# Second gather of a graph layer: one of 32 row blocks is fetched by SyncE, row by row, instead of by a GpSimd gather

## The chip, the cores and the metric

The kernel runs on one core of a Trainium2 chip. The metric is the device time of one execution in microseconds (us); lower is better. The core has five engines with a queue each: TensorE (PE, with its weight loads as PEld), VectorE (DVE), ScalarE (ACT), GpSimd (POOL) and SyncE (SP). SP computes nothing: it issues transfers and waits on semaphores. Its sequencer's work, like that of the other engines, is marked with a q (SPq).

## The reference, cut to what matters

The reference normalises 12,500 node rows of 256 floats, adds two branches to them, and then a layer of experts:

```python
def _gcn_layer(x, W, b, edge_weight, edge_src, edge_dst):
    support = x @ W
    msgs = support[edge_src] * edge_weight[:, None]
    agg = jax.ops.segment_sum(msgs, edge_dst, num_segments=N_NODES)
    return agg + b
...
h = jax.nn.elu(_gcn_layer(x, W1, b1, edge_weight, edge_src, edge_dst))
h = jax.nn.elu(_gcn_layer(h, W2, b2, edge_weight, edge_src, edge_dst))
...
xn = _layernorm(x, axis=-1)
x = x + _L0_gnn_ref(xn, ...) + _L0_mix_ref(xn[None], ...)[0]
x = x + _L0_ffn_ref(_layernorm(x, axis=-1)[None], ...)[0]
```

There are 212,500 edges, sorted by their destination. A graph layer fetches a source row of 1 KB for every edge, weighs it and adds it to its destination's row. The mix branch (`_L0_mix_ref`) is a linear attention with a two-layer network over all nodes.

## The kernel before, in words

The program is a chain of stages: `prepare` (layer norm and tables), `gather` for the first graph layer, `gather` for the second, `route`, `scatter` and `experts`. The change touches the second `gather`.

A gather stage goes through the edges in 104 turns of 2048 edges. A turn has 16 slots, each a block of 128 rows, one per partition. Turns alternate between two buffers, `u` = 0 (even turns) and `u` = 1 (odd turns); all loops run over pairs of turns, 52 in all. In a turn:

- POOL waits until the turn's indices are there (`idx_loaded`) and until its row buffer is free (`rows_used`), then issues one indirect transfer for each slot (line 451). `rows_used` of a buffer is raised by PE's first product of the next turn, so POOL can fill a buffer only while PE works on the other.
- DVE builds selection matrices `sel` (line 403) from the edges' destinations and weights.
- PE multiplies rows by selections (line 395) for four windows of four slots each, into `sums`. Ahead of the first and third windows it waits for that half of the turn's rows. Between the windows it does pieces of the mix branch and of the dense part of a finished node tile; after the fourth it does the hidden layer of the mix (line 983).
- DVE adds the four windows into `agg` (line 409), then raises `turn_added` (line 508), on which PE waits before the next turn's first window.
- SP, in its own turn, waits until all rows of the buffer's last turn have landed (line 421), loads the next indices (line 422), loads the next tile of the mix, stores the mix's result (lines 915 to 918: wait for the result, store, wait for the store, release the result buffer), and then stores and loads for the dense part (lines 1268 to 1276). It issues eight transfers in a turn.

No scheduler is at work: each engine's order is the order in which its block is written.

Of the kernel before, what the change touches and what calls it, by code (L numbers as in the profile page):

```python
# [6 lines left out]
I32 = mybir.dt.int32  # L7
# [5 lines left out]
P = 128  # L13
# [40 lines left out]
AGG = SPARE + WIN  # L54
TABLES = "natural_log_exp_and_others"
LOG_WIN = 6
LOG_TB = 8
# [32 lines left out]
def load_values(nc, engine, of, most):  # L90

    return nc.values_load_multi_w_load_instructions(of, engines=(engine,), min_val=0, max_val=most)[1]


# [15 lines left out]
def prepare(nc, m):  # L110

    with ExitStack() as ctx:
# [68 lines left out]
        with nc.Block("prepare") as block:  # L181
# [41 lines left out]
            @block.gpsimd  # L223
            def _(pool):
                nc.gpsimd.memset(m.zeros[:, :], 0.0).then_inc(zero_set, 1)
                nc.gpsimd.memset(m.ones[:, :], 1.0).then_inc(zero_set, 1)
                nc.gpsimd.iota(iota_i[:, :], [[1, WIN]], base=0, channel_multiplier=0).then_inc(iotas_done, 1)
                nc.gpsimd.iota(node_i[:, :], [[P, NT]], base=0, channel_multiplier=1).then_inc(iotas_done, 1)
                nc.gpsimd.iota(taken[:, :], [[0, 1]], base=(1 - LAG) * P, channel_multiplier=P).then_inc(taken_ready, 1)
                pool.wait_ge(zero_set, 2)  # L230

                nc.gpsimd.affine_select(out=m.ident[:, :], in_=m.zeros[:, 0:P], compare_op=ALU.not_equal, fill=1.0,
                                        base=0, pattern=[[-1, P]], channel_multiplier=1).then_inc(iotas_done, 1)
                nc.gpsimd.affine_select(out=m.upto[:, :], in_=m.ones[:, :], compare_op=ALU.is_ge, fill=0.0,
                                        base=0, pattern=[[1, P]], channel_multiplier=-1).then_inc(iotas_done, 1)
# [12 lines left out]

            @block.vector
            def _(dve):  # L250
# [54 lines left out]
                normalise(loops - 1, PSLOTS - 1, False)  # L305
                dve.wait_ge(iotas_done, 4)
                nc.vector.tensor_copy(m.cols[:, :], iota_i[:, :]).then_inc(tables_done, 1)
# [33 lines left out]

def gather(nc, m, layer, source, mixer, denser):

# [3 lines left out]
    with ExitStack() as ctx:  # L347
# [22 lines left out]
        sums = ps("sums", TURN * KD, WIN).rearrange("p (g k) w -> p g k w", g=TURN)  # L370

        idx_loaded = [sem(f"idx_loaded{u}_") for u in range(2)]
        rows_loaded = [[sem(f"rows_loaded{u}{b}_") for b in range(BANKS)] for u in range(2)]
        rows_used = [sem(f"rows_used{u}_") for u in range(2)]
# [36 lines left out]
        with nc.Block(f"gather{layer}") as block:  # L411
            @block.sync
            def _(sp):
                for u in range(2):
                    sp.dma_start(idx[:, u, :], m.in_src[u]).then_inc(idx_loaded[u], 16)
                    mix.load(sp, u, u)
                mix.load_weights(sp)
                dense.load_weights(sp)

                def turn(i, u):  # L420
                    sp.wait_ge(rows_loaded[u][BANKS - 1], 16 * GROUP * SUB * i)
                    sp.dma_start(idx[:, u, :], m.in_src[bass.ds(2 * i + u, 1)].rearrange("o p c -> (o p) c")
                                 ).then_inc(idx_loaded[u], 16)
                    mix.free(sp, i - 1, u)
                    mix.load(sp, 2 * i + u, u)
                    mix.store(sp, i - 1, u)
                    dense.sp(sp, i - 1, u)

                for i in range(1, dense.peeled):
                    for u in range(2):  # L430
                        turn(i, u)
                with sp.Fori(dense.peeled, loops) as i:
                    for u in range(2):
                        turn(i, u)
                mix.load_past(sp)
                for u in range(2):
                    dense.sp(sp, loops - 1, u)
                mix.stored(sp)
# [93 lines left out]
            def _(pe):  # L532
# [5 lines left out]
                def turn(i, u):  # L538
# [6 lines left out]
                    for g in range(TURN):  # L545
                        if g % SUB == 0:
                            pe.wait_ge(rows_loaded[u][g // SUB], 16 * GROUP * SUB * (i + 1))
# [175 lines left out]
def keys_values(nc, m, sb, sem, ps, shared):  # L723
# [110 lines left out]
    mix.dve, mix.act, mix.after = dve, act, after  # L834
    mix.store = lambda sp, i, u: None
    mix.load_weights = load_weights
# [4 lines left out]
def attend(nc, m, sb, sem, ps, shared):  # L841
# [70 lines left out]

    def store(sp, i, u):
        t = 2 * i + u
        sp.wait_ge(mixed, t + 1)
        sp.dma_start(m.mix[bass.ds(t * P, P), :], result[:, u, :]).then_inc(stored[u], 16)
        sp.wait_ge(stored[u], 16 * i + 16)
        sp.sem_inc(result_free[u], 1)

    def load_past(sp):  # L920
# [4 lines left out]
    def all_stored(sp):  # L925
        for u in range(2):
            store(sp, TURNS // 2 - 1, u)

# [183 lines left out]

    mix.load, mix.free, mix.store, mix.stored = load, free, store, all_stored
    mix.pe_begin, mix.pe, mix.pe_end = pe_begin, pe, pe_end
# [314 lines left out]
def route(nc, m):  # L1429


    with ExitStack() as ctx:
# [27 lines left out]
        spare_i = sb("spare_i", [P, NT], I32)  # L1460
        spare_f = sb("spare_f", [P, NT])
        blocks_i = sb("blocks_i", [1, NE], I32)
        blocks_f = sb("blocks_f", [1, NE])
# [17 lines left out]
        with nc.Block("route") as block:  # L1481
            @block.gpsimd
            def _(pool):
                nc.gpsimd.iota(left_i[:, :], [[-1, NE]], base=NE, channel_multiplier=0).then_inc(iotas, 1)
                nc.gpsimd.iota(spare_i[:, :], [[P, NT]], base=TRASH, channel_multiplier=1).then_inc(iotas, 1)
# [7 lines left out]
            def _(pe):  # L1493
                pe.wait_ge(chosen_ready, 1)
                for k in range(2):
                    half = chosen[:, k * HALF:(k + 1) * HALF, :]

                    nc.tensor.matmul(nth_ps[k], m.upto[:, :], half, start=True, stop=True)
                    nc.tensor.matmul(count_ps[k], m.ones[:, :], half, start=True, stop=True).then_inc(counted, 1)

            @block.vector
            def _(dve):
                count = [0]

                def link(instruction):
# [7 lines left out]
                                        ALU.subtract).then_inc(shifted, 1)  # L1513
                dve.wait_ge(iotas, 2)
                nc.vector.tensor_copy(left_f[:, :], left_i[:, :])
# [379 lines left out]
def program(nc, ins, out, scratch):  # L1895
    m = Memory()
    (m.x, m.in_src, m.in_dst, m.in_dst_rows, m.in_wgt, m.in_w_g1, m.in_b_g1, m.in_w_g2, m.in_b_g2,
     m.in_w_q, m.in_w_k, m.in_w_v, m.in_w_m, m.in_w_1, m.in_w_2, m.in_ln1_g, m.in_ln1_b, m.in_ln2_g, m.in_ln2_b,
# [12 lines left out]
    with ExitStack() as ctx:  # L1911
# [15 lines left out]
        m.ident = sb("ident", [P, P])  # L1927
        m.upto = sb("upto", [P, P])
        m.ones = sb("ones", [P, P])
# [16 lines left out]
        with ExitStack() as agg_ctx:  # L1946
            m.agg = agg_ctx.enter_context(nc.sbuf_tensor("agg", [P, KD, AGG], F32))
            gather(nc, m, 1, m.xn, keys_values, dense_first)
            gather(nc, m, 2, m.h1, attend, dense_second)
        m.row = sb("row_of", [P, NT], I32)  # L1950
# [51 lines left out]
```

## Time and profile before

| what | us |
|---|---|
| median of 3 runs (5253.92 to 5268.12) | 5263.27 |
| the profiled execution, its own time | 5257.51 |
| span of its trace, first to last instruction | 5255.6 |

The span is what the trace shows, and the 1.9 us beside it lie outside of the trace. The second gather's products run from about 2300 to 4425 us of the span. The stretch from 2500 to 4200 us is taken below as its steady part.

### The profile page before, as it was taken

How to read it: one execution, taken by the hardware profiler on the slowest of the kernel's cores; microseconds unless marked ns; L12 is line 12 of the kernel's file. 1: busy time of each engine (PE TensorE's matmuls, PEld its weight loads, DVE VectorE, ACT ScalarE, POOL GpSimd, SP SyncE). 2: the span in 40 equal slices, each digit the busy share in tenths (PEclk: the TensorE clock that was granted, in tenths of full speed). 3: DMA queues.
4: the chain of work that ended last, by engine and by line, in shares of the span. 5: the costliest groups of instructions: out<-in, count | busy, mean ns of one | idle time of the engine just before them, and what ended most of it. 6: DMA issues, size and time to landing. Idle time of an engine off the chain costs nothing. (4 is left out here: it accounts for less than half of the span.)

```text
span 5255.6 us, 89454 instructions
## 1 busy us (share of the span) xinstructions
PE 4074.3 (78%) x25266; PEld 3747.3 (71%) x25267; DVE 2650.4 (50%) x9578; ACT 814.5 (15%) x2507; POOL 3445.0 (66%) x3639
## 2 busy tenths in 40 slices
PE   0577777777777777769988999898989987069998
PEld 0467666666667776758888888888888886058886
DVE  7433333333333333355676666767666666234444
ACT  2001111111111111111222222222222222011111
POOL 0577777777777777757777777777777774632222
PEclk9867777777777777778999999999999998589999
DMA  7444444444444444434555454555545553632221
GB/s 212 142 128 132 130 132 132 130 132 130 132 131 133 132 130 132 129 89 125 147 147 152 143 151 145 147 149 146 151 144 148 147 146 109 188 112 70 67 70 65
DMA packets 409075, 693.81 MB, mean 132 GB/s; under 512 B 108237, under 2 KB 275661, under 8 KB 408893
## 3 DMA queue, kind: packets, MB, share of 16 engines
q0 software_dynamic: 177312, 488.43, 32.8%
q1 hardware_dynamic: 195765, 163.17, 10.6%
q10 hardware_dynamic: 35920, 41.25, 2.2%
q8 instruction: 40, 0.66, 0.0%
q14 instruction: 38, 0.31, 0.0%
HBM read 562.84 MB, written 129.68 MB: 132 GB/s over the span
## 5 line engine op out<-in xcount | busy, mean ns | idle before, releaser
L395 PEld LDWEIGHTS sums<-sel,rows 128*128 128x128 f32 x13312 | 1888.7, 222 | 768.0 <-DMA rows<-xn,idx 440.8
L395 PE MATMUL sums<-sel,rows 128*128 128x64 f32 x13312 | 1894.5, 305 | 672.9 <-DMA rows<-xn,idx 354.6
L451 POOL DMA_INDIRECT rows<-xn,idx x1664 | 1577.8, 948 | 642.4 <-issue 630.8
L451 POOL DMA_INDIRECT rows<-h,idx x1664 | 1585.3, 953 | 578.5 <-issue 528.9
L403 DVE TENSOR_SCALAR sel<-cols,rel_now,wgt_now 128x64 f32<-128x64 f32 x3360 | 780.4, 336 | 7.8
L409 DVE TENSOR_TENSOR agg<-agg,sums 128x128 f32 x832 | 240.3, 289 | 783.9 <-issue 604.7
L603 DVE TENSOR_TENSOR pre<-z,b_g 128x256 f32<-128x256 f32 x98 | 41.6, 424 | 526.8 <-PE z L598 526.8
L1807 PE MATMUL y_ps<-w,e_hidden 128*128 128x256 f32 x1248 | 286.1, 389 | 0.0
L1795 PE MATMUL e_hidden_ps<-tokens_t,w 128*128 128x256 f32 x1248 | 279.2, 381 | 4.4 <-DVE e_hidden L1864 3.6
L983 PE MATMUL hidden_ps<-xt,w 128*128 128x128 f32 x1664 | 265.2, 282 | 17.2 <-ACT msg_t L1104 17.0
L1735 POOL DMA_INDIRECT out<-y_result,target_i x80 | 79.5, 994 | 291.3 <-DVE y_result L1849 271.3
L1795 PEld LDWEIGHTS e_hidden_ps<-tokens_t,w 128*128 128x128 f32 x1248 | 237.5, 191 | 40.0 <-DVE e_hidden L1864 6.6
L1807 PEld LDWEIGHTS y_ps<-w,e_hidden 128*128 128x128 f32 x1248 | 241.8, 196 | 33.3
L983 PE MATMUL hidden_ps<-msg_t,w 128*128 128x128 f32 x1664 | 254.2, 275 | 0.0
L983 PEld LDWEIGHTS hidden_ps<-xt,w 128*128 128x128 f32 x1664 | 221.3, 193 | 35.3 <-ACT msg_t L1104 35.3
L946 PE MATMUL row_ps<-w,hidden 128*128 128x256 f32 x832 | 223.6, 418 | 2.7 <-ACT hidden L1108 2.7
L983 PEld LDWEIGHTS hidden_ps<-msg_t,w 128*128 128x128 f32 x1664 | 219.7, 192 | 0.0
L779 PE MATMUL kv_proj<-w_k,kv_xt 128*128 128x256 f32 x416 | 210.0, 660 | 0.0
L795 DVE TENSOR_SCALAR k_min<-kv_proj 128x256 f32<-128x256 f32 x104 | 44.1, 424 | 302.3 <-PE kv_proj L779 302.3
L946 PEld LDWEIGHTS row_ps<-w,hidden 128*128 128x128 f32 x832 | 170.1, 215 | 26.1 <-ACT hidden L1108 2.9
L971 PE MATMUL row_ps<-w_m,msg_t 128*128 128x256 f32 x416 | 125.4, 426 | 71.2 <-ACT msg_t L1096 71.2
L779 PE MATMUL kv_proj<-w_v,kv_xt 128*128 128x256 f32 x416 | 174.8, 567 | 0.0
(211 smaller groups left out, 4547.4 us busy)
## 6 DMA issues: line engine op xcount, KB each, us to landing
xe<-zeros ACTq DMA_DIRECT2D x104, 258.0 KB, 4.1
rows<-xn,idx POOLq DMA_INDIRECT x1664
rows<-h,idx POOLq DMA_INDIRECT x1664
w<-in_ffn_w POOLq DMA_DIRECT2D x16, 1024.0 KB
tile<-xn SPq DMA_DIRECT2D x105, 128.0 KB
ln_rows<-in_x SPq DMA_DIRECT2D x52, 256.0 KB
xn<-ln_normed ACTq DMA_DIRECT2D x52, 256.0 KB, 4.4
kv_tile<-xn SPq DMA_DIRECT2D x104, 128.0 KB
```

The source lines that it names most:

```text
L395: last = nc.tensor.matmul(sums[:, g, h, :], rows[:, u, k, h * P:(h + 1) * P], sel[:, u, k, :], start=(c == 0), stop=(c == GROUP - 1))
L403: last = nc.vector.tensor_scalar(sel[:, u, k, :], m.cols[:, :], rel_now[:, u, k:k + 1], wgt_now[:, u, k:k + 1], ALU.is_equal, ALU.mult)
L409: return nc.vector.tensor_tensor(window, window, sums[:, g, :, :], ALU.add)
L451: nc.gpsimd.indirect_dma_start(out=rows[:, u, k, :], out_offset=None, in_=source, in_offset=bass.IndirectOffsetOnAxis(ap=idx[:, u, k:k + 1 ...
L779: last = nc.tensor.matmul(proj[n][:, 0, :], xt[:, k, :], w[:, k, :], start=(k == 0), stop=(k == KD - 1))
L795: nc.vector.tensor_scalar(k_min[:, :], proj[0][:, 0, :], 0.0, None, ALU.min).then_inc(k_min_ready, 1)
L946: last = nc.tensor.matmul(row_ps[1], hidden[:, o, :], m.w_2[:, o, :], start=(o == 0), stop=(o == F1 // P - 1))
L971: last = nc.tensor.matmul(row_ps[0], msg_t[:, k, :], m.w_m[:, k, :], start=(k == 0), stop=(k == KD - 1))
L983: last = nc.tensor.matmul(hidden_ps[:, o, :], m.w_1[:, k, o * P:(o + 1) * P], of, start=(k == 0), stop=(k == 2 * KD - 1))
L1735: nc.gpsimd.indirect_dma_start(out=m.out, out_offset=bass.IndirectOffsetOnAxis(ap=target_i[:, tt:tt + 1], axis=0), in_=result[:, tt, :], i ...
L1795: last = nc.tensor.matmul(hidden_ps[f % HB], w1[u][:, k, f * P:(f + 1) * P], tokens_t[:, k, :], start=(k == 0), stop=(k == KD - 1))
L1807: last = nc.tensor.matmul(y_ps[tt], hidden[:, f, tt * P:(tt + 1) * P], w2[u][:, f, :], start=(f == 0), stop=(f == FC - 1))
```

## The change

Of the 32 slots of a pair of turns, POOL gathers 31. The last slot of the odd turn is fetched by SP: it reads 16 indices at a time from a 128-entry row in SBUF (`near_idx`) into its registers, computes an address from each, and issues a transfer of one row (1 KB) to one partition, 128 times in a pair. The first 64 rows are issued in SP's even turn, after a wait for the odd buffer to be free and for `near_idx`; the other 64 in its odd turn. Both stand right behind the load of the next indices, so the odd half also stands behind the wait for the odd turn's gathers. PE waits for the 128 rows (`near_loaded`) ahead of the last window of the odd turn. SP's store of the mix result is that of the turn before, and its release of the result buffer moves to the end of the turn, as `release`. A table (`upto`) moves from `prepare` to `route`.

```diff
+NEAR = 16
+HALF_ROWS = P // 2
...
+def load_rows(nc, engine, of, most):
+
+    values = nc.values_load_multi_w_load_instructions(of, engines=(engine,))[1]
+    return [value.with_bounds(min_val=0, max_val=most) for value in values]
...
+        near_idx = sb("near_idx", [1, P], I32) if by_row else None
+        far = [SLOTS, SLOTS - 1 if by_row else SLOTS]
+        last_bank = [16 * (far[u] - GROUP * SUB) for u in range(2)]
...
+                def near_rows(j, u):
+
+                    if u == 0:
+                        sp.wait_ge(rows_used[1], j + 1)
+                        wait_apart(sp, near_idx_loaded, 16 * j + 16, m.sp_passed)
+                    for k in range(u * HALF_ROWS, (u + 1) * HALF_ROWS, NEAR):
+                        ids = load_rows(nc, mybir.EngineType.SP, near_idx[0:1, k:k + NEAR], N - 1)
+                        for n in range(NEAR):
+                            sp.dma_start(rows[k + n:k + n + 1, 1, SLOTS - 1, :], source[bass.ds(ids[n], 1), :]
+                                         ).then_inc(near_loaded, 16)
+                    if u == 1:
+                        at = j * (2 * SLOTS) + (3 * SLOTS + far[1])
+                        sp.dma_start(near_idx[:, :], m.in_src_rows[bass.ds(at, 1), :]).then_inc(near_idx_loaded, 16)
+
                 def turn(i, u):
-                    sp.wait_ge(rows_loaded[u][BANKS - 1], 16 * GROUP * SUB * i)
+                    sp.wait_ge(rows_loaded[u][BANKS - 1], last_bank[u] * i)
                     sp.dma_start(idx[:, u, :], m.in_src[bass.ds(2 * i + u, 1)].rearrange("o p c -> (o p) c")
                                  ).then_inc(idx_loaded[u], 16)
+                    if by_row:
+                        near_rows(i - 1, u)
                     mix.free(sp, i - 1, u)
                     mix.load(sp, 2 * i + u, u)
                     mix.store(sp, i - 1, u)
                     dense.sp(sp, i - 1, u)
+                    mix.release(sp, i - 1, u)
...
-                        for k in range(SLOTS):
+                        for k in range(far[u]):
                             nc.gpsimd.indirect_dma_start(
...
+                        if by_row and u == 1 and g == TURN - 1:
+                            wait_apart(pe, near_loaded, 16 * P * (i + 1), m.pe_passed)
                         last = window_products(g, u, rows_used[1 - u] if g == 0 else None)
...
-    def store(sp, i, u):
+    def behind(i, u):
+        return (i, 0) if u else (i - 1, 1)
+
+    def store_tile(sp, i, u):
         t = 2 * i + u
         sp.wait_ge(mixed, t + 1)
         sp.dma_start(m.mix[bass.ds(t * P, P), :], result[:, u, :]).then_inc(stored[u], 16)
+
+    def free_result(sp, i, u):
         sp.wait_ge(stored[u], 16 * i + 16)
         sp.sem_inc(result_free[u], 1)
```

SP's queue, in the loop of the second gather, at the start of an even turn before. The names are destination and source of each transfer; an ISA row is register arithmetic.

```order
L422 ISA
L422 DMA idx<-in_src 128x16
L911 ISA
L907 ISA
L907 DMA tile<-xn 128x256
L916 ISA
L916 DMA mix<-result 128x256
```

The same place in the changed kernel: the load of 16 indices, and the first four of 64 rows.

```order
L450 ISA
L450 DMA idx<-in_src 128x16
L68 ISA
L99 TENSOR_LOAD near_idx
L442 ISA
L442 DMA rows<-h 1x256
L442 ISA
L442 DMA rows<-h 1x256
```

Between the load of the indices and that of the tile there are now 4 loads of 16 indices, and 64 pairs of an ISA row and a transfer of one row.

The end of the even turn and the start of the odd one in SP's queue of the changed kernel:

```order
L947 ISA
L947 DMA tile<-xn 128x256
L958 ISA
L959 ISA
L959 DMA mix<-result 128x256
...
L1322 DMA x_in<-in_x 128x256
L1323 DMA mix_in<-mix 128x256
L962 ISA
L449 REGISTER_ALU
L450 ISA
L450 DMA idx<-in_src 128x16
L99 TENSOR_LOAD near_idx
```

The eight transfers of before still stand in each turn, in the order of before but for the 64 rows. The odd turn's 64 rows come behind its load of indices (L450), which waits for the gathers of the odd turn.

POOL's loop of the second gather, before and then in the changed kernel:

```order
L451 DMA rows<-h,idx 128x256 x32
```

```order
L488 DMA rows<-h,idx 128x256 x31
```

POOL issues one gather less in a pair; the first gather's loop keeps its 32.

## Rows read from the trace of the kernel before

**Rows 1.** The page's head: span, then busy time of each engine.

```profile
span 5255.6 us, 89454 instructions
PE 4074.3 (78%) x25266; PEld 3747.3 (71%) x25267; DVE 2650.4 (50%) x9578; ACT 814.5 (15%) x2507; POOL 3445.0 (66%) x3639
```

**Rows 2.** Busy time by stretch: first gather, second gather; columns in its first line.

```profile
core 0: us, PE busy (x) PEld busy (x) DVE busy (x) ACT busy (x) POOL busy (x), PEclk, DMA share, GB/s
1000.00:1500.00 500.00, 373.73 (x2046) 345.12 (x2045) 176.63 (x674) 51.70 (x150) 378.44 (x400) 0.75 0.47 132
2500.00:4200.00 1700.00, 1530.23 (x11278) 1432.30 (x11276) 1165.94 (x4397) 381.70 (x1327) 1266.51 (x1329) 0.95 0.51 148
```

**Rows 3.** Groups by line on POOL, 2500 to 4200 us: count | busy, mean ns | idle.

```profile
L451 POOL DMA_INDIRECT rows<-h,idx x1329 | 1266.6, 953 | 433.6 <-issue 418.7 <-DMA idx<-in_src 8.8 <-PE sums L395 6.1
```

**Rows 4.** Waits, 2500 to 4200 us: us in total, times, longest.

```profile
POOL rows L451 <- issue: 418.7, 1280, 3.6
PE sums L395 <- DVEq L508: 87.7, 74, 2.1
PEld sums L395 <- DMA rows<-h,idx: 3.8, 3, 1.7
PE sums L395 <- DMA rows<-h,idx: 2.0, 2, 1.5
```

**Rows 5.** Timeline of POOL, two gathers in a row: start, us, idle before.

```profile
3013.12 0.95 POOL L451 DMA_INDIRECT rows<-h,idx  x1 [0.30 <-DMA idx<-in_src]
3014.37 0.95 POOL L451 DMA_INDIRECT rows<-h,idx  x1 [0.30 <-issue]
```

**Rows 6.** Timeline of PE, an odd turn and the next turn's first window.

```profile
3013.05 1.97 PE L395 MATMUL sums<-sel,rows 128*128 128x64 f32 x16 [0.44 <-DVEq L508]
...
3024.74 1.89 PE L395 MATMUL sums<-sel,rows 128*128 128x64 f32 x16
...
3031.22 0.61 PE L983 MATMUL hidden_ps<-msg_t,w 128*128 128x128 f32 x4
3033.55 1.99 PE L395 MATMUL sums<-sel,rows 128*128 128x64 f32 x16 [1.71 <-DVEq L508]
```

**Rows 7.** SP's own waits, 2500 to 4200 us: us in total, times, longest.

```profile
SPq L916 <- DVE result L1031: 1139.7, 83, 18.1
SPq L918 <- DMA mix<-result: 170.0, 83, 2.3
```

**Rows 8.** Timeline of SP, the transfers of a turn: start, us it took to issue.

```profile
3024.01 0.35 SPq L916 DMA_DIRECT2D mix<-result  x1
3027.16 0.35 SPq L1273 DMA_DIRECT2D x<-x_now  x1
...
3029.29 0.40 SPq L1269 DMA_DIRECT2D mix_in<-mix  x1
3029.89 0.33 SPq L422 DMA_DIRECT2D idx<-in_src  x1
3030.48 0.33 SPq L907 DMA_DIRECT2D tile<-xn  x1
```

**Rows 9.** Single lines' instructions: duration ns min/median/max (L422: 2500 to 4200 us).

```profile
L422 SPq FUSED_REGOPS  x83: 52/52/57, 2514.4 to 4196.9; - x83
L422 SPq MOVE idx<-in_src x83: 29/29/29, 2514.5 to 4197.0; - x83
L422 SPq DMA_DIRECT2D idx<-in_src x83: 332/337/343, 2514.6 to 4197.1; - x83
L1595 SPq DMA_DIRECT2D s_rows<-xf x42: 372/373/383, 4488.4 to 4591.2; - x42
L1691 SPq TENSOR_LOAD <-blocks x18: 254/258/282, 4617.9 to 5212.1; - x18
L92 DVEq TENSOR_LOAD <-table x416: 352/536/1737, 187.7 to 4421.7; - x139
```

**Rows 10.** Queues: packets, MB, share of 16 DMA engines' span (q1 carries SP's transfers).

```profile
q1 hardware_dynamic: 195765, 163.17, 10.6%
```

More of the change, by code:

```diff
@@ L339, in _, with gather @@
                 dve.wait_ge(tables_done, 15)
-def gather(nc, m, layer, source, mixer, denser):
+def gather(nc, m, layer, source, mixer, denser, by_row):
     with ExitStack() as ctx:
@@ L416, in _ @@
                     mix.load(sp, u, u)
+                if by_row:
+                    sp.dma_start(near_idx[:, :], m.in_src_rows[SLOTS + far[1]:SLOTS + SLOTS, :]).then_inc(near_idx_loaded, 16)
                 mix.load_weights(sp)
                 dense.load_weights(sp)
+                def near_rows(j, u):
[10 more added lines that the diff above has]
+                        sp.dma_start(near_idx[:, :], m.in_src_rows[bass.ds(at, 1), :]).then_inc(near_idx_loaded, 16)
                 def turn(i, u):
-                    sp.wait_ge(rows_loaded[u][BANKS - 1], 16 * GROUP * SUB * i)
+                    sp.wait_ge(rows_loaded[u][BANKS - 1], last_bank[u] * i)
                     sp.dma_start(idx[:, u, :], m.in_src[bass.ds(2 * i + u, 1)].rearrange("o p c -> (o p) c")
                                  ).then_inc(idx_loaded[u], 16)
+                    if by_row:
+                        near_rows(i - 1, u)
                     mix.free(sp, i - 1, u)
@@ L434, in _ @@
                         turn(i, u)
+                if by_row:
+                    for u in range(2):
+                        near_rows(loops - 1, u)
+                    wait_apart(sp, near_idx_loaded, 16 * loops + 16, m.sp_passed)
                 mix.load_past(sp)
                 for u in range(2):
+                    mix.store(sp, loops - 1, u)
                     dense.sp(sp, loops - 1, u)
+                    mix.release(sp, loops - 1, u)
                 mix.stored(sp)
@@ L834, in keys_values @@
     mix.dve, mix.act, mix.after = dve, act, after
-    mix.store = lambda sp, i, u: None
+    mix.store = mix.release = lambda sp, i, u: None
     mix.load_weights = load_weights
@@ L916, in store, with release @@
         sp.dma_start(m.mix[bass.ds(t * P, P), :], result[:, u, :]).then_inc(stored[u], 16)
+    def free_result(sp, i, u):
         sp.wait_ge(stored[u], 16 * i + 16)
         sp.sem_inc(result_free[u], 1)
+    def store(sp, i, u):
+        if not before_first(i, u, 1):
+            store_tile(sp, *behind(i, u))
+    def release(sp, i, u):
+        if not before_first(i, u, 1):
+            free_result(sp, *behind(i, u))
     def load_past(sp):
@@ L925, in all_stored @@
     def all_stored(sp):
-        for u in range(2):
-            store(sp, TURNS // 2 - 1, u)
+        store_tile(sp, TURNS // 2 - 1, 1)
+        free_result(sp, TURNS // 2 - 1, 1)
     def turn_tile(pe, t, u, i):
@@ L1111, in act_end @@
         guess_sd(act, TURNS - 1, 1)
-    mix.load, mix.free, mix.store, mix.stored = load, free, store, all_stored
+    mix.load, mix.free, mix.store, mix.release, mix.stored = load, free, store, release, all_stored
     mix.pe_begin, mix.pe, mix.pe_end = pe_begin, pe, pe_end
@@ L1461, in route @@
         spare_f = sb("spare_f", [P, NT])
+        upto = sb("upto", [P, P])
         blocks_i = sb("blocks_i", [1, NE], I32)
@@ L1483, in _ @@
             def _(pool):
+                nc.gpsimd.affine_select(out=upto[:, :], in_=m.ones[:, :], compare_op=ALU.is_ge, fill=0.0,
+                                        base=0, pattern=[[1, P]], channel_multiplier=-1).then_inc(iotas, 1)
                 nc.gpsimd.iota(left_i[:, :], [[-1, NE]], base=NE, channel_multiplier=0).then_inc(iotas, 1)
@@ L1496, in _ @@
                     half = chosen[:, k * HALF:(k + 1) * HALF, :]
-                    nc.tensor.matmul(nth_ps[k], m.upto[:, :], half, start=True, stop=True)
+                    nc.tensor.matmul(nth_ps[k], upto[:, :], half, start=True, stop=True)
                     nc.tensor.matmul(count_ps[k], m.ones[:, :], half, start=True, stop=True).then_inc(counted, 1)
@@ L1927, in program @@
         m.ident = sb("ident", [P, P])
-        m.upto = sb("upto", [P, P])
         m.ones = sb("ones", [P, P])
@@ L1947, in program @@
             m.agg = agg_ctx.enter_context(nc.sbuf_tensor("agg", [P, KD, AGG], F32))
-            gather(nc, m, 1, m.xn, keys_values, dense_first)
-            gather(nc, m, 2, m.h1, attend, dense_second)
+            gather(nc, m, 1, m.xn, keys_values, dense_first, False)
+            gather(nc, m, 2, m.h1, attend, dense_second, True)
         m.row = sb("row_of", [P, NT], I32)
@@ L1977 @@
         "src": padded(src, NCH * P).reshape(TURNS, SLOTS, P).transpose(0, 2, 1),
+        "src_rows": padded(src, (NCH + 2 * SLOTS) * P).reshape(NCH + 2 * SLOTS, P),
         "dst": columns(dst_padded),
```

13 lines of the change are left out of this document (7 added, 6 removed).

## The prediction

> **What bounds the kernel now.** I read the page's head first. PE is busy for 78% of the span and POOL for 66% [rows 1], but these are averages over stages, so I took the busy times by stretch. In the second gather PE is busy for 1530 of 1700 us at a granted clock of 0.95, and POOL for 1267 [rows 2]. POOL's line looks like the limit: 1329 gathers in 1700 us, 0.95 us each, and nearly all of its idle time is "issue" [rows 3], the 0.30 us between two gathers [rows 5]. So a gather costs POOL 1.25 us, 16 of them 20.0 us, and a turn lasts 16 × 1700 / 1329 = 20.47 us, a pair 40.9 us.
>
> The waits say who needs POOL, and that is where the reader should look twice. PE waits for rows from POOL for 2.0 us (its weight loads for 3.8 us) in all 83 turns, and for DVE's `turn_added` (L508) for 87.7 us [rows 4]. PE's first window waits for DVE, not for rows, also in the timeline [rows 6]. So POOL is nearly full, but its rows arrive before PE wants them; the pair is held by the loop between PE and DVE. Taking a gather from POOL can give at most a little. What the change costs is then a question for SP. SP now idles for most of a turn: 1139.7 us of its 1700 go to the wait for the mix's result, 170.0 to that store's landing [rows 7].
>
> **What the change removes.** 52 gathers of 1.25 us leave POOL, 65 us in all. By the waits above nothing of it lies on the path in the steady part; I count it as 0.
>
> **What it adds: the price of a row on SP.** Each of 128 rows in a pair costs SP an address computation, a register move and an issue. The first two, with the gaps between, can be read between two transfers: the load of `mix_in` ends at 3029.29 + 0.40 = 3029.69, that of `idx` starts at 3029.89, and between them stand one FUSED_REGOPS and one MOVE [rows 8, 9]. That is 0.20 us. The issue of one row stands nowhere in the trace. From above it is bounded by the cheapest issue there, 0.33 us for 128 rows of 64 bytes; from below by a bare register move, 0.03 us [rows 9]. The upper end is the nearer row, because it is the same instruction on the same sequencer, and because its price hardly depends on the rows it moves: 256 rows take 0.373, 128 take 0.337, which leaves 0.30 for none. A row that goes to one partition could still spare some of what a spread over 128 partitions costs, so I take 0.25. A row is then 0.45 us, with ends 0.23 and 0.53.
>
> The loads of 16 indices: one value took SP 0.26 us, two or four took DVE 0.54 in the median [rows 9]. Ends are 0.26 and 16 × 0.26 = 4.1 us; I take 0.75, near the short loads, so 4 of them are 3.0 us in each half.
>
> SP's other eight transfers of a turn stay. Without the wait for the store's landing they are seven from 3027.16 to 3030.81 and the store of the mix, 0.35 [rows 8]: 4.0 us, and with the register work ahead of the first of each and the loop's branch I use 4.6. The store of the mix result a turn later removes its wait: the result is then a turn old. The release, now behind five more issues (over 2 us), finds the store landed, since that took 170.0 / 83 = 2.05 us [rows 7]. Both cost nothing as long as SP is what is late; if SP were early, the wait for the result would again be idle time of SP, which nobody pays for.
>
> **Where it lies on the path.** The new wait stands ahead of PE's fourth window of the odd turn. Behind it on PE are that window, the mix's hidden layer and the next turn; behind these are DVE's adds, `rows_used`, POOL's next odd gathers and SP's next even half. On SP the new wait for `rows_used` has the next tile's load, the store of the mix and the dense transfers queued behind it. PE and DVE want these a turn or more later, and with a longer pair that turn is longer too, so I cost it at nothing as long as the last rows are later still. All this closes a loop through SP, and I sum it from the issue of the last row (X) of one pair to that of the next:
> - the row lands: an issue of 0.36 and a landing like that of the mix store, 2.05; 2.4 us.
> - PE's fourth window and what follows up to the hidden layer's end: from 3024.74 to 3031.83 [rows 6], 7.1 us. DVE's adds go on beside it. With 0.3 for the semaphores, 7.4 us to the next even turn's first window, which frees the odd buffer.
> - SP sees it: 0.4 us, my estimate. Its own eight transfers (4.6 us) of the odd turn are done by then, beside the last two points.
> - the even half: 3.0 + 64 × 0.45 = 31.8 us.
> - SP's transfers of the even turn, and the next `idx`: 4.6 us.
> - the odd half: 31.8 us. Its wait for POOL's odd gathers is over: they start 1.2 us or so after that first window, take 14 × 1.25 + 0.95 = 18.5 us and land some 2 us later, 21.7 in all, and SP gets there at 0.4 + 31.8 + 4.6 = 36.8 us.
>
> The sum is 2.4 + 7.4 + 0.4 + 31.8 + 4.6 + 31.8 = 78.4 us for a pair, against 40.9. SP is then the limit: 128 rows at 0.45 us are 57.6 us by themselves, more than a whole pair of now. 52 pairs × 37.5 us = 1950 us, on top of the profiled execution's 5257.5 us: 7207, so 7210 us. The median of the runs shown is 6 us above that execution, which is nothing here.
>
> With the issue at 0.33 the pair is 10.2 + 6.0 + 128 × 0.53 + 4.6 = 88.6 us, and the time 5257.5 + 52 × 47.7 = 7740 us. PE would also lose its clock when it idles for half of a pair: in the first gather, busy for 75%, it was granted 0.75 [rows 2]. At that, 7.1 us become 9.5, another 2.4 × 52 = 125 us; I keep it for the upper end. At the lower end, 0.23 a row, the pair is 10.2 + 6.0 + 29.4 + 4.6 = 50.2 us, and the time 5740 us.
>
> **Edits at nothing.** The load of `near_idx` is one more issue in 78 us, beside PE's tail. `upto` is one short instruction of POOL, at another place. The bytes are the same, and a packet of SP's queue takes 0.106 × 16 × 5255.6 / 195765 = 0.046 us of a DMA engine [rows 10], so even on a single one 128 rows are 6 us in 78.
>
> **Rivals.**
> - *A cheap issue* (0.05 to 0.18 us for one row). For it: one row needs one descriptor, where the cheapest issue of now covers 128. Against it: the slope over rows above. At 0.10 a row is 0.30 us, and the pair 10.2 + 6.0 + 38.4 + 4.6 = 59.2 us: 5257.5 + 52 × 18.3 = 6210 us.
> - *The rows fit in SP's idle time, and it isn't slower.* The place that decides is the odd half: rows of the odd turn land 21.7 us after the even turn's first window, that is about 1.5 to 2 us into an odd turn of now, and the fourth window starts 11.7 us into it [rows 6]. With 0.5 for `idx`, 3.0 for the loads and 2.4 to land, some 4 us are left for 64 rows, 0.06 us each (0.09 if the loads cost 0.26 each). The register work alone is 0.20, so this needs a sequencer three times as fast as its rows show. What it would give is small: PE's waits for rows are 2 to 6 us in the steady part, and a little at the start, so 5240 us, the same. The Trainium skill ("DMA: Bandwidth & Descriptors", section "Issuing engines are not separate DMA queues") says that issuing from several engines at once saves only the sequencer's time, and calls that small beside the transfer; by that rule this rival would be the likeliest. The trace disagrees for rows this small, with 0.33 us to issue against 0.046 us for a packet.
> - *Loads value by value, or a queue that fills up.* At 4.1 us a load of 16 indices, each half is 13.4 us longer: the pair is 105 us and the time 8600 us. Two and four values at 0.54 speak against a price by the value; back-to-back issues that grow from 0.35 to 0.40 [rows 8] speak a little for a queue that pushes back.
>
> **How the numbers follow.** The likeliest, an issue of 0.18 to 0.33 us with SP as the limit, has a chance of 0.58; the cheap issue 0.30; that it fits 0.04; the slow loads or a full queue 0.06; the rest 0.02. The predicted time is 7210 us. The range goes from 5900, an issue of 0.05 with a little for landings, to 7800, an issue of 0.33 with half of the lost clock. It leaves out what fits, what is far slower, and the very cheap end of the cheap issue, some 0.15 together. The measurement of this kernel tells about 0.3% from no change; of the cases only the one that fits isn't slower, so faster 0.02, same 0.02, slower 0.96.
>
> **What would show it.** In the changed profile: 1612 gathers of `h` on POOL instead of 1664; 6656 transfers of one row on SP, whose median is the issue that I could not read (right: 0.18 to 0.33 us); a pitch of 0.4 to 0.5 us between them; a wait of PE for `rows` from SP ahead of the fourth window, once in a pair, of some 30 us; POOL's waits moved from "issue" to PE; a pair of 70 to 90 us; and a granted clock well under 0.95 in this stage. The prediction is wrong if the rows are issued in under 0.1 us each, and wrong in its mechanism if the pair grows while SP waits for something in its half turns.

## The result

The changed kernel takes 7330.44 us in the median of 4 runs (7323.29 to 7332.57). The kernel before, run beside it, takes 5259.25 us. The ratio is 1.3933, with a 95% interval of 1.3909 to 1.3958: slower by 2071 us, or 39.8 us in each of 52 pairs of turns. The prediction was 7210 us, so it is off by 120 us in 2071.

The profiled execution took 7331.24 us. First its page: the span and the busy times, three groups of instructions (count | busy, mean ns | idle before, and what ended it), the issues of rows, and SP's queue.

```profile
span 7329.5 us, 110266 instructions
PE 4317.1 (59%) x25266; PEld 3971.5 (54%) x25267; DVE 2660.3 (36%) x9578; ACT 829.2 (11%) x2507; POOL 3399.7 (46%) x3587
...
q1 hardware_dynamic: 209183, 170.04, 7.9%
...
L407 PE MATMUL sums<-sel,rows 128*128 128x64 f32 x13312 | 2013.9, 318 | 1996.8 <-DMA rows<-h 1424.1
...
L488 POOL DMA_INDIRECT rows<-h,idx x1612 | 1539.5, 955 | 2646.9 <-PE sums L407 1938.5
...
L986 PE MATMUL tile_ps<-ident,tile 128*128 128x128 f32 x210 | 56.7, 363 | 601.0 <-DMA tile<-xn 601.0
...
rows<-h SPq DMA_DIRECT2D x6656, 1.0 KB
```

No engine computes much longer than before [rows 1]; PE's 243 us more are the same 25266 instructions at a lower clock (0.736 granted in the mean of the span, 0.850 before). What is new is idle time: PE waits 1424 us for rows that come from SP, and POOL, whose idle time was "issue" before [rows 3], now waits 1938 us for PE to free a buffer. The window of 3900 to 6300 us, with 30 pairs, shows the same as waits (us in total, times, longest):

```profile
POOL rows L488 <- PE sums L407: 1262.5, 38, 42.6
...
DVE agg L421 <- PE sums L407: 885.1, 29, 32.3
...
PE sums L407 <- DMA rows<-h: 811.2, 29, 29.7
...
PE tile_ps L986 <- DMA tile<-xn: 316.2, 30, 10.8
```

PE waits twice in a pair: about 10.5 us for the tile of the mix, and about 28 us for SP's rows. DVE and POOL wait behind it. SP's own wait in the same window is short:

```profile
SPq L68 <- PE sums L407: 118.9, 30, 4.7
```

4.0 us a pair: for the other 77 SP waits for nobody. Its timeline over one pair shows with what (start, time to the end of the last of the group):

```profile
3987.92 30.60 SPq L442 DMA_DIRECT2D rows<-h  x64
4018.81 0.36 SPq L947 DMA_DIRECT2D tile<-xn  x1
...
4023.44 0.33 SPq L450 DMA_DIRECT2D idx<-in_src  x1
4025.15 30.40 SPq L442 DMA_DIRECT2D rows<-h  x64
4055.76 0.23 SPq L446 DMA_DIRECT2D near_idx<-in_src_rows  x1
...
4059.49 0.38 SPq L1323 DMA_DIRECT2D mix_in<-mix  x1
4062.89 0.34 SPq L450 DMA_DIRECT2D idx<-in_src  x1
4067.94 1.15 SPq L442 DMA_DIRECT2D rows<-h  x3
```

This pair is 4067.94 − 3987.92 = 80.0 us, and 61.0 of them are rows, with six of their eight loads of indices. The issue of the odd half's last row ends at 4055.55. PE takes over 1.1 us later:

```profile
4056.67 3.65 PE L407 MATMUL sums<-sel,rows 128*128 128x64 f32 x16 [29.36 <-DMA rows<-h]
...
4065.31 0.61 PE L1037 MATMUL hidden_ps<-msg_t,w 128*128 128x128 f32 x4
4065.99 1.99 PE L407 MATMUL sums<-sel,rows 128*128 128x64 f32 x16
```

The window that follows a wait of 29 us takes 3.65 us, where it took 1.89 before [rows 6]: PE comes out of the wait at the lower of its two clock levels, 1.2 GHz. Over the window of 3900 to 6300 us the granted clock is 0.71 (the third number from the end), where it was 0.95 before [rows 2]:

```profile
3900.00:6300.00 2400.00, 1241.15 (x8135) 1156.99 (x8134) 848.85 (x3176) 284.86 (x958) 889.20 (x930) 0.71 0.26 76
```

The single instructions of a row, and the load of 16 indices (ns, minimum/median/maximum):

```profile
L442 SPq FUSED_REGOPS  x3807: 37/37/47, 3906.4 to 6299.9; - x191
L442 SPq MOVE rows<-h x3807: 29/29/37, 3906.5 to 6300.0; - x191
L442 SPq DMA_DIRECT2D rows<-h x3806: 224/228/309, 3906.5 to 6299.6; - x191
...
L99 SPq TENSOR_LOAD <-near_idx x416: 1134/1228/1431, 2304.6 to 6465.7; - x139
```

One row takes 0.228 us to issue. Three of a half's four loads lie inside of its 30.60 us, at 1.3 us with the gaps around each, so a row's pitch is (30.60 − 0.23 − 3 × 1.3) / 63 = 0.42 us, and 0.19 us of it is register work and gaps.

### The profile page after: what moved, and what is told of

Its sections match the earlier page's. It is cut to its first block and busy times, and to the rows that moved or that the text cites. A ratio compares the mean times of both kernels' runs of the same rounds, so it can differ in the third digit from the quotient of the medians.

```text
span 7329.5 us, 110266 instructions
## 1 busy us (share of the span) xinstructions
PE 4317.1 (59%) x25266; PEld 3971.5 (54%) x25267; DVE 2660.3 (36%) x9578; ACT 829.2 (11%) x2507; POOL 3399.7 (46%) x3587
## 5 line engine op out<-in xcount | busy, mean ns | idle before, releaser
L407 PE MATMUL sums<-sel,rows 128*128 128x64 f32 x13312 | 2013.9, 318 | 1996.8 <-DMA rows<-h 1424.1
L407 PEld LDWEIGHTS sums<-sel,rows 128*128 128x128 f32 x13312 | 2006.2, 235 | 2117.1 <-issue 1660.2
L488 POOL DMA_INDIRECT rows<-h,idx x1612 | 1539.5, 955 | 2646.9 <-PE sums L407 1938.5
L986 PE MATMUL tile_ps<-ident,tile 128*128 128x128 f32 x210 | 56.7, 363 | 601.0 <-DMA tile<-xn 601.0
L986 PEld LDWEIGHTS tile_ps<-ident,tile 128*128 128x128 f32 x210 | 28.6, 174 | 614.1 <-DMA tile<-xn 614.1
L1045 DVE BATCH_NORM_STATS2 stats<-row_ps 128x6 f32<-128x256 f32 x208 | 88.7, 427 | 548.9 <-PE row_ps L1025 499.8
L1037 PE MATMUL hidden_ps<-xt,w 128*128 128x128 f32 x1664 | 282.7, 297 | 0.2
L1158 ACT ACTIVATE msg_t<-turn_ps,ln_b,ln_gh 128x128 f32<-128x128 f32 x208 | 83.8, 453 | 1607.1 <-PE turn_ps L1030 1607.1
L1852 PEld LDWEIGHTS e_hidden_ps<-tokens_t,w 128*128 128x128 f32 x1248 | 238.9, 192 | 39.9 <-DVE e_hidden L1921 6.7
L1037 PEld LDWEIGHTS hidden_ps<-xt,w 128*128 128x128 f32 x1664 | 244.6, 211 | 10.1 <-ACT msg_t L1158 10.1
L1000 PE MATMUL row_ps<-w,hidden 128*128 128x256 f32 x832 | 196.7, 380 | 0.7 <-ACT hidden L1162 0.7
```

The lines of the kernel that those rows point to most:

```text
L407: last = nc.tensor.matmul(sums[:, g, h, :], rows[:, u, k, h * P:(h + 1) * P], sel[:, u, k, :], start=(c == 0), stop=(c == GROUP - 1))
L488: nc.gpsimd.indirect_dma_start(out=rows[:, u, k, :], out_offset=None, in_=source, in_offset=bass.IndirectOffsetOnAxis(ap=idx[:, u, k:k + 1 ...
L986: last = nc.tensor.transpose(tile_ps[:, h, :], tile[:, u, h * P:(h + 1) * P], m.ident[:, :])
L1000: last = nc.tensor.matmul(row_ps[1], hidden[:, o, :], m.w_2[:, o, :], start=(o == 0), stop=(o == F1 // P - 1))
L1037: last = nc.tensor.matmul(hidden_ps[:, o, :], m.w_1[:, k, o * P:(o + 1) * P], of, start=(k == 0), stop=(k == 2 * KD - 1))
L1045: nc.vector.bn_stats(stats[:, n, :], row_ps[n]).then_inc(ln_step[n], 1)
```

## The experiments

My theory: SP's instructions for 128 rows stand one after another in a loop with PE's last window, and nothing else in the change costs or gives anything. The rivals: the new order of SP's stores costs too; a gather less on POOL is a gain that the rows hide; the bytes, not the instructions, take the time; the wait for the tile is part of it.

**reorder_only.** The second gather is called with `by_row` false.

```diff
-            gather(nc, m, 2, m.h1, attend, dense_second, True)
+            gather(nc, m, 2, m.h1, attend, dense_second, False)
```

> The changed kernel with the second gather told to fetch all 32 row blocks through GpSimd's queue again: SyncE's turn keeps its new order, with the store of the mix a turn later and its release at the turn's end, and the moved triangle of ones. Theory 1 (SyncE's row by row issue is the whole price): as the kernel before, 5250 to 5270 us. Rival (the new order of stores and releases costs too): over 5300 us.

Measured: 5266.1 us, ratio 1.0016 (1.0007 to 1.0025). The reordering, with the moved table, costs 7 us. The rest of the 2071 us comes with the rows.

**no_rows.** POOL's 31 gathers stay, SP's rows and PE's wait for them go.

```diff
-                    if by_row:
-                        near_rows(i - 1, u)
...
-                        if by_row and u == 1 and g == TURN - 1:
-                            wait_apart(pe, near_loaded, 16 * P * (i + 1), m.pe_passed)
```

> Nobody fetches the 32nd row block: GpSimd issues 31 gathers a pair of turns, SyncE issues no row and TensorE waits for none; the block stays zero, so its 128 edges are left out. Theory 1 (a gather taken from GpSimd is worth next to nothing, because TensorE and VectorE hold each other up as long as the gathers take): 5235 to 5262 us. Rival (GpSimd's gathers set the turn): 1.25 us saved in each of 52 pairs, about 5195 us.

Measured: 5269.43 us, ratio 1.0021 (1.0012 to 1.003), the same as reorder_only. So 65 us of gathers taken from POOL are worth nothing by themselves.

**plain_loads** starts from the kernel before and shortens the other limit that the rows of before name, the loop between PE and DVE [rows 4]. In both gathers it leaves out the bound tests of the four window positions that DVE loads in a turn.

```diff
-                    low = load_values(nc, mybir.EngineType.DVE, m.table[0:1, bass.ds(t, 1), 0:TURN], N - 1)
+                    low = load_rows(nc, mybir.EngineType.DVE, m.table[0:1, bass.ds(t, 1), 0:TURN], N - 1)
```

> The kernel before with one edit: VectorE loads the four window positions of a turn without the bound tests that take about 0.28 us each between its last sum and its adds, about 1.1 us a turn in each of the two gathers. Theory 1 (the turn is held jointly by GpSimd's 16 gathers of 1.25 us, 20.0 us, and by a loop between TensorE and VectorE of 20.2 us): faster by 0.2 to 0.25 us in 104 turns of one or both gathers, 5205 to 5240 us. Rival (VectorE's loads are not on the path): 5250 to 5270 us. Rival (GpSimd's gathers are no limit): about 5140 us or less.

Measured: 5233.06 us, ratio 0.9948 (0.9934 to 0.9961). This version is 0.5% faster than the kernel before, and so faster than both.

**plain_no_rows** does both.

> Both edits at once: nobody fetches the 32nd row block of the second gather (its 128 edges are left out), and VectorE loads its window positions without bound tests in both gathers. Theory 1 (two limits that stand side by side, so that taking either away alone gives little): more than the two gains apart, 5130 to 5200 us. Rival (either limit alone sets the time): the sum of the two gains at most.

Measured: 5170.73 us, ratio 0.9832 (0.9817 to 0.9847). The waits from 2500 to 4200 us tell the story of the three. In no_rows PE still waits for DVE, and POOL waits for PE:

```profile
PE sums L407 <- DVEq L539: 108.8, 78, 2.4
...
POOL rows L480 <- PE sums L407: 55.6, 37, 2.9
```

In plain_loads that wait of PE, 87.7 us before [rows 4], is small, and its weight loads wait for rows:

```profile
PEld sums L401 <- DMA rows<-h,idx: 69.0, 65, 2.4
...
PE sums L401 <- DVEq L514: 17.5, 18, 1.3
```

In plain_no_rows it is again POOL's rows that PE waits for, and POOL has no time left but between gathers (its longest "issue" gap is 0.3 us, where it was 3.6 before [rows 4]):

```profile
PE sums L407 <- DMA rows<-h,idx: 44.4, 52, 1.4
...
L480 POOL DMA_INDIRECT rows<-h,idx x1348 | 1289.6, 957 | 410.7 <-issue 408.9 <-PE sums L407 1.8
```

POOL and the PE–DVE loop are two limits side by side. With DVE's loads short, POOL's 52 gathers are worth 5233.06 − 5170.73 = 62 us, 1.2 us each, their full price; with the long loads they are worth nothing.

**one_load.** One load of 16 indices for a half, used four times.

```diff
-                    for k in range(u * HALF_ROWS, (u + 1) * HALF_ROWS, NEAR):
-                        ids = load_rows(nc, mybir.EngineType.SP, near_idx[0:1, k:k + NEAR], N - 1)
+                    ids = load_rows(nc, mybir.EngineType.SP, near_idx[0:1, 0:NEAR], N - 1)
+                    for k in range(u * HALF_ROWS, (u + 1) * HALF_ROWS, NEAR):
```

> The changed kernel with one load of 16 indices per half turn in place of four; the same 16 rows are fetched in all four groups, so the rows are wrong. Issues and register arithmetic stay. Theory 1 (SyncE's instructions stand one after another on the path of each pair, a load of 16 indices among them at 1.23 us): 6 x 1.23 = 7.4 us less in each of 52 pairs, 6930 to 6970 us. Rival (SyncE's loads run beside the queue's work, and the rows' transfers set the time): 7280 us or more.

Measured: 6463.12 us, 867 us less than the changed kernel, more than twice what I expected. The trace says why:

```profile
L442 SPq MOVE rows<-h x3978: 29/29/37, 3512.2 to 5499.9; - x199
L442 SPq DMA_DIRECT2D rows<-h x3978: 224/225/323, 3512.2 to 5500.0; - x199
L442 SPq FUSED_REGOPS  x1002: 37/37/43, 3512.1 to 5499.8; - x167
```

There is one address step (FUSED_REGOPS) for four rows: the program keeps the addresses of the 16 rows, so my edit took away 96 address steps of a pair as well as 6 loads. With the gap beside it a step is 0.09 us: the rows that have one follow each other in 0.41 us, the others in 0.32. The sum, 6 × 1.23 + 96 × 0.09 = 16.0 us a pair, or 833 us, stands beside the 867 measured. The price by the instruction holds; the expectation was wrong about what the edit removes.

**static_rows.** Fixed rows, without loads and addresses.

```diff
-                        ids = load_rows(nc, mybir.EngineType.SP, near_idx[0:1, k:k + NEAR], N - 1)
                         for n in range(NEAR):
-                            sp.dma_start(rows[k + n:k + n + 1, 1, SLOTS - 1, :], source[bass.ds(ids[n], 1), :]
+                            sp.dma_start(rows[k + n:k + n + 1, 1, SLOTS - 1, :], source[k + n:k + n + 1, :]
```

> The changed kernel with each of the 128 rows fetched from a fixed place: no index is loaded and no address worked out, so the rows are wrong; 128 one-row transfers stay. Theory 1 (SyncE's time per row is 0.18 us of register work and 0.225 us of issue): the pitch falls from 0.41 to 0.23 to 0.30 us, a half turn to 15 to 19 us, the pair to 46 to 57 us, so 5540 to 6100 us. Rival (the transfers themselves take their 0.4 us a row): above 6800 us.

Measured: 5977.01 us, 13.8 us a pair above before, so 54.7 us a pair. The issue stays:

```profile
L441 SPq DMA_DIRECT2D rows<-h x3526: 222/252/320, 3500.0 to 4999.7; - x196
```

A row follows the other in 0.30 us in place of 0.42. With 8 loads of 1.3 us less that is 25.8 us a pair, and 26.0 were measured. Even with everything else gone, 128 issues of one row cost more than SP and PE can hide.

**tiny_rows.** 64 bytes of each row in place of 1024.

```diff
-                            sp.dma_start(rows[k + n:k + n + 1, 1, SLOTS - 1, :], source[bass.ds(ids[n], 1), :]
+                            sp.dma_start(rows[k + n:k + n + 1, 1, SLOTS - 1, 0:16], source[bass.ds(ids[n], 1), 0:16]
```

> The changed kernel with 16 of the 256 values of each row fetched, 64 bytes in place of 1024; the other columns of the block stay zero. As many transfers, loads and address steps. Theory 1 (the price is SyncE's instructions, not the bytes or the memory): 7300 to 7350 us. Rival (the transfer of a row takes part in the 0.41 us between two rows): a pitch under 0.35 us and under 7000 us.

Measured: 7320.56 us, and the issue of a row takes what it took with 1024 bytes:

```profile
L442 SPq DMA_DIRECT2D rows<-h x3815: 224/228/310, 3906.0 to 6299.7; - x191
```

The bytes don't matter. The Trainium skill ("DMA: Bandwidth & Descriptors", section "Issuing engines are not separate DMA queues") calls the sequencer's time to issue usually small beside the transfer. This case doesn't agree for rows of 1 KB: a sixteenth of the bytes left the time where it was, so here the sequencer's time is the price.

**half_rows.** The even half alone.

```diff
-                    for k in range(u * HALF_ROWS, (u + 1) * HALF_ROWS, NEAR):
+                    for k in range(0, HALF_ROWS if u == 0 else 0, NEAR):
...
-                            wait_apart(pe, near_loaded, 16 * P * (i + 1), m.pe_passed)
+                            wait_apart(pe, near_loaded, 16 * HALF_ROWS * (i + 1), m.pe_passed)
```

> The changed kernel with the first 64 of the 128 rows alone, in the even turn; the other 64 edges of the block stay zero. Theory 1 (both halves stand in one loop with TensorE's last window): one half and SyncE's transfers around it leave the loop, which then is 31.7 us of rows and 10 to 14 us to the next first window, 41 to 46 us a pair against 40.9 before: 5270 to 5520 us. Rival (half of the added 2075 us stays, the price being a sum over rows alone): about 6300 us.

Measured: 5803.83 us, 51.3 us a pair, outside of what either theory gave. The waits of 3000 to 4400 us show a wait that I had costed at nothing:

```profile
PE tile_ps L988 <- DMA tile<-xn: 268.6, 27, 10.4
```

PE waits 10 us a pair for the tile of the mix, whose transfer stands behind the 64 rows on SP. The wait stands behind the second window of the odd turn. The third still comes before the window of the rows, and by then they have landed: PE has no wait for them in this stretch.

**half_tile_between.** The tile's transfer goes out after 32 of the 64 rows.

```diff
+                        if k == u * HALF_ROWS + 2 * NEAR:
+                            midway()
...
+                    def next_tile():
+                        mix.free(sp, i - 1, u)
+                        mix.load(sp, 2 * i + u, u)
+
...
-                        near_rows(i - 1, u)
-                    mix.free(sp, i - 1, u)
-                    mix.load(sp, 2 * i + u, u)
+                        near_rows(i - 1, u, next_tile)
```

> The kernel with the first 64 rows alone (the other 64 edges of the block stay zero), which took 5804 us, with one step moved: the transfer of the next turn's tile of the mix is issued after 32 of the 64 rows in place of behind all of them. Theory 1 (the rows hold up the tile transfer behind them on SyncE, TensorE waits about 10 us a pair for it, and this is the part of the time that the halved rows did not explain): the tile lands in time, a pair is 31.7 us of rows and 11 to 15 us behind them, 43 to 47 us: 5370 to 5580 us. Rival (the pair of 51.4 us comes from something else, such as TensorE's clock or GpSimd's gathers): 5750 us or more.

Measured: 5531.23 us, 45.9 us a pair. The wait for the tile is gone from that window, and a short one for the rows takes its place:

```profile
PE sums L407 <- DMA rows<-h: 69.7, 26, 3.4
```

So 5.4 of the 10.4 us that half_rows added to a pair were the tile's. The other 5.0 come with the rows, and not as waits alone: 2.3 us a pair are PE's waits for rows, and PE is busy for 39.2 us a pair (1194.10 of 1400, at a granted clock of 0.90) in place of 36.8 (1530.23 of 1700, at 0.95 [rows 2]).

**tile_between.** The same move in the full kernel.

> The changed kernel with the same step moved, in both turns of a pair: the tile's transfer goes out after 32 of a turn's 64 rows. Theory 1 (in the full kernel TensorE's wait of about 10 us a pair for the tile lies beside its wait for the second half's rows, and SyncE issues the same instructions in all): within 0.3 per cent of 7330 us. Rival (the tile wait is a part of the added time): 10 us less in each of 52 pairs, about 6800 us.

Measured: 7368.41 us, ratio to before 1.398 (1.394 to 1.4021), where the changed kernel has 1.3933: not faster, if anything 0.3% slower by these ratios, and 38 us by the times as they are (the kernel before, run beside it, took 5272.26 us). That is at or just outside the edge of the 0.3% expected. PE's waits for rows, 3500 to 5000 us, and PE behind one of them:

```profile
PE sums L407 <- DMA rows<-h: 779.8, 19, 41.3
...
3910.31 3.64 PE L407 MATMUL sums<-sel,rows 128*128 128x64 f32 x16 [41.20 <-DMA rows<-h]
...
3920.89 1.99 PE L407 MATMUL sums<-sel,rows 128*128 128x64 f32 x16
```

The wait for the tile didn't go away; it joined the wait for rows, 41 us in place of 28 and 10.5. From the start of this window to the next first window PE takes 10.6 us here, and 10.3 in the mean of 27 pairs (9.1 to 10.8); in the changed kernel the pair shown took 9.3, and the mean is 10.1 (9.3 to 10.7), so the longer wait costs little of its own. What the move does cost is read from SP: in the odd turn the tile's transfer stood behind the last row, beside PE's work, and now stands among the rows, so that the odd half takes 30.98 us in place of 30.40. That is 0.58 us a pair, or 30 us in 52, and it leaves SP earlier at its wait for PE, which grew from 4.0 to 4.8 us a pair (144.9 us in 30).

**free_at_summed.** SP's even half starts when the odd buffer has been read, not when the next turn begins.

```diff
-                        sp.wait_ge(rows_used[1], j + 1)
+                        if not before_first(j, 0, 1):
+                            sp.wait_ge(summed, 2 * j)
```

> The changed kernel with one wait moved: SyncE's rows of a pair start when TensorE has finished the odd turn's sums, in place of the first product of the turn behind it. Theory 1 (SyncE and TensorE take turns in one loop): the 6 to 9 us between the two events leave the loop of each of 52 pairs: 6860 to 7020 us. Rival (SyncE's own work fills the pair, or the rows start no earlier since SyncE is busy): 7300 us or more.

Measured: 7120.24 us, 210 us or 4.0 us a pair less than the changed kernel, short of the 6 to 9 expected. 4.0 us is just what SP waited for PE in the changed kernel. After this SP has no regular wait left in a pair of some 77 us (80.8 less 4.0), and the rest of the gap between the two events is filled by SP's transfers and by 3 us at the end of its loop:

```profile
4007.23 0.35 SPq L1324 DMA_DIRECT2D mix_in<-mix  x1
4008.04 0.33 SPq L451 DMA_DIRECT2D idx<-in_src  x1
...
4044.18 0.38 SPq L1324 DMA_DIRECT2D mix_in<-mix  x1
4047.62 0.34 SPq L451 DMA_DIRECT2D idx<-in_src  x1
```

From `mix_in` to `idx` SP takes 0.46 us inside the pair and 3.06 us where the loop goes back. In static_rows and half_rows, whose loops are shorter, it takes 0.7 to 0.8 us there.

**long_loop** asks whether that is the length of the loop: before's SP loop, lengthened by instructions that do nothing.

```diff
+                    if layer == 2:
+                        for n in range(125):
+                            sp.sem_inc(m.passed, 1)
```

> The kernel before with one edit: in the second gather SyncE raises an unused semaphore 125 times at the end of each of its turns, so that its loop over pairs holds about 303 instructions in place of 53; POOL gathers all 32 blocks and no row is fetched by SyncE. Theory 1 (the 2.4 us that SyncE loses at the end of its loop in the changed kernel come with the length of the loop's code): from the last instruction of the odd turn to the load of the indices behind it SyncE loses 2 to 4 us in place of 0.6, and the page's instruction queue shows some 270 to 290 packets in place of 38. Rival (they come with the rows, such as a queue of SyncE that is full): 0.6 us and about 38 packets. The time stays at 5240 to 5290 us if 250 such instructions fit into the 31 us of a pair in which SyncE only waits, and grows if they don't.

Measured: 5496.95 us; the instructions don't fit in SP's idle time, since they delay the indices and the tile behind them: from 2500 to 4200 us POOL waits 199.9 us for indices, where it was 8.8 before, and PE 144.3 us for the tile. The loop's end, then the odd turn's start:

```profile
3024.38 0.35 SPq L1272 DMA_DIRECT2D mix_in<-mix  x1
3036.03 0.34 SPq L422 DMA_DIRECT2D idx<-in_src  x1
...
3043.16 0.41 SPq L1272 DMA_DIRECT2D mix_in<-mix  x1
3051.55 0.34 SPq L422 DMA_DIRECT2D idx<-in_src  x1
```

The same 125 instructions stand between both, but the stretch with the loop's end is 11.30 us and the other 7.98: 3.3 us more, without any row. The trace has it between the branch that closes the loop and SP's next instruction, 3.2 us for the first and for the last pair of these rows (start of the first and of the last):

```profile
L435 SPq COMPARE_BRANCH  x45: 45/50/56, 2573.0 to 4597.4; - x45
L435 SPq FUSED_REGOPS  x45: 46/46/46, 2576.2 to 4600.6; - x45
```

The page's instruction queue agrees, for long_loop, for the changed kernel, and for the kernel before, in this order:

```profile
q14 instruction: 276, 2.25, 0.2%
```

```profile
q14 instruction: 285, 2.33, 0.1%
```

```profile
q14 instruction: 38, 0.31, 0.0%
```

So the 3 us come with the length of the code.

## Why the prediction was right, step by step

- *What the change removes is worth 0.* Right, and shown by no_rows beside reorder_only. plain_no_rows shows the condition: only as long as the loop between PE and DVE takes as long as the gathers.
- *Register work 0.20, issue 0.25 a row.* Measured 0.19 and 0.23. The bound from below was close to nothing and the one from above 0.33; the guess that one row spares part of the cost of 128 was right, and the cheap issue (0.05 to 0.18) is excluded.
- *A load of 16 indices 0.75.* Mis-sized: 1.23. The loads that I had, of 0.26 and 0.54 us, were of one to four values, and I leaned too far to them. Over 8 loads this is +3.8 us a pair, and 128 rows at 0.03 to 0.04 us less are some −4 to −5: the half of 31.8 us was met (1.3 + 30.6, and 1.3 + 30.4) by two errors that cancel, which was luck.
- *SP's other transfers 4.6.* From the last even row to the first odd one it is 6.6 us; without the first load, 1.3, that is 5.3. Off by 0.7.
- *The last row lands in 2.4.* PE starts 1.1 us after the issue ends, 1.4 after it began. Off by 1.0 the other way.
- *PE's fourth window and what follows, 7.4.* Mis-sized: 9.3 in the pair shown and 10.1 in the mean, because PE starts it at half its clock after 29 us of waiting. I had seen this, at 2.4 us, and kept it for the upper end of the range; the stretch's granted clock is 0.71, where 0.95 stood before [rows 2], so it belonged in the sum.
- *SP sees it in 0.4.* From the first product at 4065.99 to the row at 4067.94 it is 1.95 us, of which a load and its gap are 1.3; 0.6 is left.

Together: 1.1 + 9.3 + 0.6 + 31.9 + 5.3 + 31.7 = 79.9 us for this pair, against 78.4 predicted and 80.8 on average (the 40.9 of before, and 39.9 more by the two profiled executions). What follows PE's wait, 9.3 us here and 10.1 in the mean, makes most of the difference to the average. The two largest errors, on the loads and on the rows, cancel; of those that are left the clock's is the largest, 1.9 us in this pair and 2.7 in the mean.

- *What is queued behind the new waits costs nothing.* Right in the full kernel, where tile_between moved the tile's transfer and won nothing. But the condition that I gave, as long as the last rows are later still, was all that hid it: half_rows broke it and paid 5 us a pair for the tile. The reason beside it, that the turn or more until PE wants the tile grows with the pair, was wrong: PE wants it in the middle of the odd turn, before SP is through the 64 rows ahead of it, and waits 10.5 us a pair.
- *SP's odd transfers are done beside PE's tail.* Right with less room than I thought. They end at 4063.23, with the 2.5 us at the end of SP's loop that no row of before shows, and PE frees the buffer at 4065.99. free_at_summed shows what lies below: SP's own pair of some 77 us.
- *The rivals.* That the rows fit was refuted by static_rows, where even bare issues don't. A queue that pushes back: issues stay at 228 ns over 3806 rows, with a maximum of 309. tiny_rows excludes the bytes. Loads value by value, at 4.1 us for 16: they take 1.23. One reading in the working on the rows that fit was off: 21.7 us less a turn of 20.47 is 1.2 us into the odd turn, not 1.5 to 2, which would leave some 4.6 us for 64 rows and changes nothing in the outcome.

## What to carry to other kernels

Moving a gather from a queue that looks full gains nothing when its consumer waits for something else; look at who waits for the queue, and at what would be late next. A transfer per row is priced here by the issuing sequencer, per instruction, at 64 bytes as at 1024: 128 rows at 0.42 us against one gather of 1.25 us. Before rows are put into a queue's idle time, list what stands behind them there, since a tile that comes late can cost as much as the rows themselves, and disappears from sight as soon as the rows are later still.

## What the runs showed of the hardware

- SP's issue of a transfer of one row takes 0.225 to 0.228 us (0.252 from a fixed address), against 0.33 to 0.37 for 128 and 256 rows [rows 9].
- A load of 16 values into SP's registers takes 1.23 us, against 0.26 for one [rows 9]: by these two points some 0.065 us for each further value, an estimate.
- A loop of SP whose body holds 303 to 453 instructions loses 2.5 to 3.4 us where it goes back, against the same stretch inside its body; with 53, 188 and 256 instructions (before, static_rows, half_rows) it loses 0.3 to 0.4 us. The Trainium skill ("Runtime: NRT & Kernel Launch", section "Instruction fetch mechanics") says that a taken branch whose target is outside of the window of pages that the engine holds must fetch the target's page before it goes on. The runs agree with it: long_loop shows the loss and the instruction queue's 276 packets without a single row. The lengths between 256 and 303 weren't tried.
- PE's first window after a wait of 15, 28 or 41 us (static_rows, the changed kernel, tile_between) runs at the lower of its two clock levels (3.65 us in place of 1.89). How soon PE is back doesn't follow from the length of the wait: from that window to the next first window it takes 9.9, 10.1 and 10.3 us in the mean. In half_rows, after 10 us for the tile, the two windows behind took 3.5 us each in every second pair, and 2.4 and 1.9 us in the others.
